# Middle heads of an attention kernel: third group's output product ahead of the eighth tile's transposes, the last exponential later, and the sparse row summed by VectorE

## The reference, cut to what matters

```python
scores = jnp.where(causal[None, None], -jnp.inf, scores)
probs = jax.nn.softmax(scores.astype(jnp.float32), axis=-1).astype(q.dtype)
attn = jnp.einsum('bhqk,bhkd->bhqd', probs, v)
...
io = sparse_out.mean(axis=2)[:, :, None, :VD]
io = jnp.broadcast_to(io, (B, IH, S, VD))
io = jnp.repeat(io, NH // IH, axis=1)
attn = attn + io
out = attn.transpose(0, 2, 1, 3).reshape(B, S, NH * VD) @ W_o
```

## Time and profile before

| what | value |
|---|---|
| runs | 697.52, 697.83, 703.88 us; median 697.83 |
| profiled execution | 697.48 us |
| its span, first to last instruction | 695.6 us |
| mean granted TensorE clock | 0.982 of full speed |
| busy | PE 94%, DVE 67%, ACT 58%, POOL 54% |
| chain that ended last | PE 62%, DVE 12%, ACT 11%, issue 9%, POOL 3%, DMA 1% |

### The profile page before, as it was taken

How to read it: one execution, slowest core, us unless ns; L and a number is a source line. 1 busy time by engine, 2 the same in 40 slices (tenths; PEclk the granted TensorE clock), 3 DMA queues, 4 the chain that set the end, 5 groups by cost and what they waited for, 6 DMA issues and landing times.

```text
span 695.6 us, 14180 instructions
## 1 busy us (share of the span) xinstructions
PE 654.3 (94%) x4502; PEld 594.1 (85%) x4502; DVE 467.7 (67%) x1292; ACT 400.5 (58%) x934; POOL 372.8 (54%) x335
## 2 busy tenths in 40 slices
PE   8897998999999999999999999999999999889895
PEld 6786987889888988898889888998899888779895
DVE  5884466666675657575756576666667667887986
ACT  4891346564656475736574476447664758545552
POOL 6882277245662757173826384448354735541564
PEclk9996999999999999999999999999999999999998
DMA  8307032510362034212441054104610383000001
GB/s 232 111 1 182 31 62 59 131 55 1 92 147 66 0 90 110 50 51 68 96 85 53 26 114 108 53 0 105 143 53 0 90 235 98 1 1 1 1 16 46
DMA packets 23551, 49.85 MB, mean 72 GB/s; under 512 B 3168, under 2 KB 16352, under 8 KB 21600
## 3 DMA queue, kind: packets, MB, share of 16 engines
q1 hardware_dynamic: 22144, 47.82, 27.4%
q10 hardware_dynamic: 1376, 1.64, 0.7%
HBM read 16.94 MB, written 1.05 MB: 26 GB/s over the span
## 4 chain that ended last, share of the span: by engine, by line
PE 62%; DVE 12%; ACT 11%; issue 9%; POOL 3%; DMA 1%; ACTq 0%; DVEq 0%; POOLq 0%; SPq 0%
PE J L840 10%; PE J L842 9%; PE J L841 9%; PE J L873 4%; PE SC L860 3%; ACT kvraw L1253 3%; PE SC L863 3%; PE SC L861 3%; PE SC L862 3%; PE SC L864 3%; DVE PTl L1299 3%; ACT Pb L1158 3%; POOL rstd L710 3%; PE SC L1054 2%; PE SC L1055 2%
## 5 line engine op out<-in xcount | busy, mean ns | idle before, releaser
L1299 DVE TENSOR_TENSOR PTl<-J,PTh 128x512 fp32r<-128x512 f32 (+1 forms) x192 | 102.2, 553 | 65.7 <-ACT PTh L1141 65.0
L1158 ACT ACTIVATE Pb<-SC,nm 128x128 f32<-128x128 f32 (+7 forms) x128 | 94.8, 741 | 63.3 <-DVE nm L1368 62.3
L1368 DVE CUSTOM_DVE_ANT_0 SC<-SC,mask 128x128 f32<-128x128 f32 (+7 forms) x128 | 97.3, 760 | 32.3 <-PE SC L864 30.4
L873 PE MATMUL J<-ident,Pb 128*128 128x128 f32 x576 | 87.4, 279 | 5.8 <-ACT Pb L1158 5.2
L1141 ACT ACTIVATE PTh<-J 128x512 fp32r<-128x512 f32 (+1 forms) x192 | 88.2, 491 | 7.5 <-PE J L873 6.7
L840 PE MATMUL J<-PTh,Vh 128*128 128x256 f32 x320 | 87.9, 275 | 2.8 <-DVE PTl L1299 2.8
L841 PE MATMUL J<-PTl,Vh 128*128 128x256 f32 x320 | 89.5, 280 | 0.0
L842 PE MATMUL J<-PTh,Vl 128*128 128x256 f32 x320 | 89.4, 279 | 0.0
L873 PEld LDWEIGHTS J<-ident,Pb 128*128 128x128 f32 x576 | 64.4, 142 | 13.2 <-ACT Pb L1158 6.7
L860 PE MATMUL SC<-KNh,QNh 128*128 128x128 f32 (+2 forms) x192 | 69.2, 360 | 0.1
L1141 ACT ACTIVATE ATh<-J 128x256 fp32r<-128x256 f32 x64 | 24.5, 383 | 73.7 <-PE J L842 72.9
(11 more groups left out here) (310 smaller groups left out, 1912.5 us busy)
## 6 DMA issues: line engine op xcount, KB each, us to landing
KK<-RK SPq DMA_DIRECT2D x30, 512.0 KB, 6.3
QS<-RQh SPq DMA_DIRECT2D x15, 256.0 KB, 6.2
QS<-RQl SPq DMA_DIRECT2D x15, 256.0 KB, 6.1
KX<-KX SPq DMA_DIRECT2D x14, 256.0 KB, 2.3
QX<-QX SPq DMA_DIRECT2D x14, 256.0 KB, 2.4
r_kv<-in_W_ckv SPq DMA_DIRECT2D x7, 384.0 KB, 3.3
r_o<-in_W_o SPq DMA_DIRECT2D x18, 128.0 KB, 3.3
r_qn<-in_W_qT SPq DMA_DIRECT2D x16, 128.0 KB, 3.2
```

The costliest lines, as they stand in the source:

```text
L873: last = pe.transpose(o[:, tile(j - 4 * c)], Pb[i % 2][:, tile(j)], ident[:, :])
L1158: act.activation(Pb[i % 2][:, w], SC[i % 2][:, s], ACT.Exp, bias=nm[:, i % 2:i % 2 + 1], scale=-1.0, accum_out=sm[:, b, i:i + 1]).then_inc ...
L1299: dve.tensor_tensor(o, i, h.bitcast(F32), ALU.subtract).then_inc(done[kind], 1)
L1368: dve.tensor_tensor_reduce(out=SC[i % 2][:, s], in0=SC[i % 2][:, s], in1=mask[:, 128 * (7 - i):S], scale=-SCALE, scalar=HIGH, op0=ALU.add, ...
```

## The change

1. `wo` 2 of the head before stands ahead of `tc` 7 (slot 0), in every head that has one before it.
2. In odd heads of the loop (`more and not first`) the second half of the query projection, `qp` 1, moves ahead of `pv` 3.
3. In the odd heads of FIRST and MID tile 7's `exp` stands one step later, behind `pv` 2.
4. In the same odd heads of MID the second `kt` moves from the end of slot 3 to slot 4, behind `wo` 0.
5. The row product leaves PE. DVE does `row = r_o * iocol + row` in one instruction per head, element by element, on W_o as it was loaded, one partition per row of `W_o`; it no longer needs the split in high and low parts. Once, in head 15, one fp32 matmul with ones (`rwt`) sums the 128 partitions, and a DVE copy brings the result back. ("skip") keeps the bank turns. SP's `W_o` load waits for the DVE instruction two heads before; POOL's split waits for `ab` alone, and two splits that nobody reads are gone. `io` and `rw` stand earlier in the odd heads.

```diff
@@ -370,7 +367,8 @@
-            add(0, tail, *t(m, 7), ("wo", m, 2))
+            add(0, tail, ("wo", m, 2), *t(m, 7))
+            add(1, b == 1 and more and not first, ("qp", 1, 1))
             add(1, tail, ("pv", m, 3))
...
@@ -382,7 +380,7 @@
-                add(4, True, *t(h, 3), ("wo", h, 0), ("rw", n, 0))
+                add(4, True, *t(h, 3), ("wo", h, 0), ("rw", n, 0), ("skip", 0, 0))
...
@@ -396,12 +394,13 @@
                 add(0, last, ("rw", 3, 0))
+                add(1, last, ("rwt", 0, 0))
...
-                add(1, more and not first, ("qp", 1, 1), ("ropeq", 1, 0))
+                add(1, more and not first, ("ropeq", 1, 0))
...
@@ -409,19 +408,19 @@
-                add(3, more and not first, ("kt", n, 1))
                 add(3, first, ("ab", n, 0), ("kvn2", 1, 0))
                 add(4, True, *t(h, 3), ("wo", h, 0))
-                add(4, more and not first, ("ab", n, 0))
+                add(4, more and not first, ("kt", n, 1), ("ab", n, 0))
...
-                add(6, more and not first, ("io", 1, 0))
+                add(4, more and not first, ("io", 1, 0))
                 add(6, True, *t(h, 5), ("wo", h, 1))
-                add(6, more, ("rw", n, 0))
+                add(5, more, ("rw", n, 0))
+                add(6, more, ("skip", 0, 0))
...
@@ -429,7 +428,7 @@
-            exp_at = [[2, 2, 2, 2, 2, 2, 2, 2], [2, 2, 2, 2, 2, 2, 2, 2]]
+            exp_at = [[2, 2, 2, 2, 2, 2, 2, 2], [2, 2, 2, 2, 2, 2, 2, 3 if more else 2]]
...
@@ -569,7 +568,8 @@
-                    wait(sp, wo_split, u)
+                    wait(sp, wo_split, min(u, NH) if isinstance(u, int) else u)
+                    wait(sp, rw_done, u - 2)
...
@@ -730,9 +730,8 @@
-                    if kind == "wosp" and not (isinstance(u, int) and u == 0):
-                        hold(gp, ready["ab"], min(u, NH) if isinstance(u, int) else u)
-                        split(ld_o, 16 * u + 16, r_o[:, :], Woh[:, :], Wol[:, :], wo_hi, wo_split, ready["rw"], u - 2, u)
+                    if kind == "wosp" and not (isinstance(u, int) and u in (0, NH, NH + 1)):
+                        split(ld_o, 16 * u + 16, r_o[:, :], Woh[:, :], Wol[:, :], wo_hi, wo_split, ready["ab"], u, u)
...
@@ -1006,10 +1005,9 @@
-                if kind == "rw":
-                    pe.wait_ge(io_ready, p + off // 2)
-                    pe.wait_ge(wo_split, u + 1)
-                    last = three(o[:, 0:D], iocol[:, 0:1].to_broadcast([128, 128]), iocol[:, 1:2].to_broadcast([128, 128]), Woh[:, :], Wol[:, :], True, True)
+                if kind == "rwt":
+                    pe.wait_ge(rw_done, NH)
+                    last = mm(o[:, 0:D], lhsT=onesf[:, :], rhs=row[:, :], start=True, stop=True)
...
@@ -1530,20 +1528,21 @@
-                            dve.tensor_copy(ioThl[:, :, 0], ioT[:, :]).then_inc(io_hi, 1)
-                            dve.wait_ge(io_hi, 1)
-                            dve.tensor_tensor(ioThl[:, :, 1], ioT[:, :], ioThl[:, :, 0].bitcast(F32), ALU.subtract).then_inc(io_hi, 1)
-                            dve.wait_ge(io_hi, 2)
-                        pair = ioThl[:, bass.ds(u, 1), :].rearrange("p a n -> p (a n)")
-                        dve.tensor_copy(iocol[:, :], pair.bitcast(F32)).then_inc(io_ready, 1)
+                        dve.tensor_copy(iocol[:, :], ioT[:, bass.ds(u, 1)]).then_inc(io_ready, 1)
...
                     if kind == "rw":
-                        dve.wait_ge(ready["rw"], count("rw", u, 0))
-                        dve.tensor_tensor(row[:, :], o[:, 0:D], row[:, :], ALU.add).then_inc(done["rw"], 1)
+                        dve.wait_ge(io_ready, p + off // 2)
+                        dve.wait_ge(ld_o, 16 * u + 16)
+                        if not (isinstance(u, int) and u == 2):
+                            hold(dve, rw_done, u - 2)
+                        dve.scalar_tensor_tensor(row[:, :], r_o[:, :], iocol[:, 0:1], row[:, :], ALU.mult, ALU.add).then_inc(rw_done, 1)
+                    if kind == "rwt":
+                        dve.wait_ge(ready["rwt"], 1)
+                        dve.tensor_copy(row[:, :], o[:, 0:D]).then_inc(done["rwt"], 1)
                     if kind == "rowadd":
-                        dve.wait_ge(done["rw"], NH)
+                        dve.wait_ge(done["rwt"], 1)
```

More of the change, by code:

```diff
@@ L123, in attention_and_mlp @@
         ioT = sb("ioT", [128, IH])
-        ioThl = sb("ioThl", [128, IH, 2], F32R)
-        iocol = sb("iocol", [128, 2], F32R)
+        iocol = sb("iocol", [128, 1])
         row = sb("row", [128, D])
@@ L246, in attention_and_mlp @@
                  ("qc", "qm", "kv", "kpe", "qp", "qps", "kt", "ab", "qn", "pv", "wo", "side", "tc", "wb",
-                  "rw", "wtot", "ht", "h2")}
+                  "rwt", "wtot", "ht", "h2")}
         hi = {k: sem(f"{k}_hi") for k in ("xs", "kt", "ab", "qn", "vs", "pv", "tc", "ht", "h2",
@@ L253, in attention_and_mlp @@
                 ("xs", "qc", "qm", "kv", "kpe", "qp", "qps", "kt", "ab", "qn", "vs", "pv", "wo", "side", "tc",
-                 "wb", "rw", "wtot", "ht", "h2")}
+                 "wb", "rwt", "wtot", "ht", "h2")}
         ld_mlp = [sem(f"ld_mlp{n}") for n in range(3)]
@@ L283, in attention_and_mlp @@
         tp_ready, pt_lo = ready["tc"], done["tc"]
-        io_hi, io_ready = sem("io_hi"), sem("io_ready")
+        io_ready, rw_done = sem("io_ready"), sem("rw_done")
         row_added = sem("row_added")
@@ L303, in unit @@
         def unit(kind, off, p):
-            if kind in ("wtot", "ht"):
+            if kind in ("wtot", "ht", "rwt"):
                 return off
@@ L1161, in run @@
                         kind, o = "qm", J[bank_of[("qm", 0, c)]]
-                    if kind in ready and not (kind in ("side", "wb", "wtot", "wo", "rw", "h2", "qc") or
+                    if kind in ready and not (kind in ("side", "wb", "wtot", "wo", "rwt", "h2", "qc") or
                                               kind in ("qp", "qps") and isinstance(u, int) and u == 0):
@@ L1532, in run @@
                             dve.wait_ge(done["side"], 13)
-                            dve.tensor_copy(ioThl[:, :, 0], ioT[:, :]).then_inc(io_hi, 1)
-                            dve.wait_ge(io_hi, 1)
-                            dve.tensor_tensor(ioThl[:, :, 1], ioT[:, :], ioThl[:, :, 0].bitcast(F32), ALU.subtract).then_inc(io_hi, 1)
-                            dve.wait_ge(io_hi, 2)
-                        pair = ioThl[:, bass.ds(u, 1), :].rearrange("p a n -> p (a n)")
-                        dve.tensor_copy(iocol[:, :], pair.bitcast(F32)).then_inc(io_ready, 1)
+                        dve.tensor_copy(iocol[:, :], ioT[:, bass.ds(u, 1)]).then_inc(io_ready, 1)
                     if kind == "io0":
-                        dve.wait_ge(ready["rw"], NH - 2)
-                        dve.tensor_copy(iocol[:, :], ioThl[:, 0, :].bitcast(F32)).then_inc(io_ready, 1)
+                        dve.wait_ge(rw_done, NH - 2)
+                        dve.tensor_copy(iocol[:, :], ioT[:, 0:1]).then_inc(io_ready, 1)
                     if kind == "rw":
-                        dve.wait_ge(ready["rw"], count("rw", u, 0))
-                        dve.tensor_tensor(row[:, :], o[:, 0:D], row[:, :], ALU.add).then_inc(done["rw"], 1)
+                        dve.wait_ge(io_ready, p + off // 2)
[6 more added lines that the diff above has]
+                        dve.tensor_copy(row[:, :], o[:, 0:D]).then_inc(done["rwt"], 1)
                     if kind == "rowadd":
-                        dve.wait_ge(done["rw"], NH)
+                        dve.wait_ge(done["rwt"], 1)
                         dve.wait_ge(done["wo"], count("wo", NH - 2, c))
```

4 lines of the change are left out of this document (1 added, 3 removed).

## The result

The changed kernel takes 713.58 us (median of 4 runs, 711.27 to 718.41), the kernel before in the same company 699.53. The ratio is 1.0204, with a 95% interval of 1.0156 to 1.0253: slower by 1.6 to 2.5%, and outside the range of 686 to 710 that was forecast. The profiled execution takes 714.28 us with a span of 712.4, 16.8 more than before. Its mean granted clock is 0.967 instead of 0.982.

What follows compares the result with a forecast made beforehand. PE was taken to bound the kernel; -5.7 - 2.9 + 11.1 + 0 + 1.8 + 1.8 + 0.7 - 1.1 = +5.7 on 697.5 gave 703.2 us, range 686 to 710.

Steps and rivals of the forecast that it cites:

- (c): Odd-to-even head boundary, seven times: `pv` 3 starts later behind `PTl` 7b, +1.58 us each, +11.1 for seven.
- (e): Boundaries head 0 to 1 and last pair: additions ahead of the chunk add about 0.9 us each, +1.8.
- The second rival: At the seven odd-to-even boundaries PE's new idle stretch lowers its clock: 12 us more, 715 us; chance 0.07.
- (a): Row product, 16 steps of three matmuls: it leaves PE, -5.7 us.
- (b): Odd heads: PE's wait at the row product goes with it, -2.9 us.
- (d): Even-to-odd boundary, six times: projection covers `pv` 3, 0; second `kt` in odd heads +0.3 us each, +1.8.
- (f): End of program: the one fp32 matmul with DVE's copy costs +0.7 us.
- (g): Head 1: DVE's cast `ioThl` and its follower go, so PE waits less, -1.1 us.
- (h): SP and POOL: changed waits and two splits fewer, 0, covered by PE.
- The rival on POOL: All 16 DVE row instructions held up by POOL, 0.7 us each: 11 us more, 714; chance 0.03.

Runs made afterwards that it cites:

- row sum, late: Kernel before with only the row sum moved to DVE, its row instruction in slot 6 instead of 5 in odd heads: 692.03 us, ratio 0.9864.
- row sum alone: Kernel before with only the row sum moved to DVE, its row instruction in slot 5 in odd heads: 693.60 us, ratio 0.9922.
- filled kernel: Changed kernel with 10 useless score matmuls of tile 1 in even heads from head 2 on: 703.73 us, ratio 1.0081.
- late row + `wo` + exponential: Kernel before with the row sum on DVE (slot 6 in odd heads), `wo` 2 ahead of tile 7's transposes and tile 7's exponential behind `ATh` in odd heads: 704.43 us.
- late row + projection: Kernel before with the row sum on DVE (slot 6 in odd heads) and the query projection's second half ahead of `pv` 3 in middle odd heads: ratio 0.9898.

## Why the prediction was wrong, point by point

**What failed is a term that the sum put at nothing: the clock behind the new wait.** Terms (c) and (e) price PE's idle stretch at its length alone. The second rival ("PE's new idle stretch lowers its clock", 715 us) got a chance of 0.07 and is what happened: about 1.5 us behind each of the seven boundaries, 10.5 us, and a low clock behind the two of (e) as well. The profiled execution takes 714.28.

The reason given against the rival was that PE is fuller here than in head 1. That was no evidence: nothing in the rows spoke for PE's fullness as a protection. Of the two waits that the prediction compared, 1.27 us with a full clock behind it and 2.58 with a low one, the forecast 2.2 was nearer to the second. But the length alone did not settle it either. The trace of the kernel before holds two more waits, and they go the other way round, the longer with a full clock behind it, the shorter with a low one (clock third from the end):

```profile
618.06 0.63 PE L873 MATMUL J<-ident,Pb 128*128 128x128 f32 x4 [1.64 <-ACT Pb L1158]
618.00:622.00 4.00, 3.94 (x29) 3.77 (x30) 3.83 (x9) 1.49 (x3) 0.09 (x1) 1.00 0.01 4
...
647.01 0.58 PE L1054 MATMUL SC<-QNh,xTh 128*128 128x256 f32 x1 [1.45 <-DVE CS L1463]
647.00:648.00 1.00, 0.99 (x4) 0.99 (x5) 0.97 (x5) 0.77 (x2) 0.52 (x1) 0.50 0.00 0
```

So the rows called for an open chance, near one half, and not for 0.07.

**What was right, and what was luck.** The turn was forecast at 73.6 us at full clock, and the changed kernel with its idle stretch filled takes 73.63. The boundary is right as a mechanism: from `pv` 2's last matmul to `pv` 3 it grew by 1.57 us, forecast 1.58. That the whole turn agrees to 0.03 is luck, for the parts miss by -0.34 to +0.22 and cancel.

| step | predicted | measured | from |
|---|---|---|---|
| (a), (b) row product and its waits, per turn | -1.10 | -0.88 | row sum, late: 71.92 against 72.80 |
| (c) `wo` and exponential, per turn | +1.58 | +1.24 | 73.16 against 71.92 |
| (d) projection, per turn | 0 | -0.01 | 71.91 against 71.92 |
| (d) second `kt`, per turn | +0.3 | +0.39 | 72.31 against 71.92 |
| low clock, per turn | 0 (rival: +1.7) | +1.5 | 75.12 against 73.63; 74.74 against 73.16 |
| (f) fp32 product | +0.7 | +0.25 | 626.51 to 626.76 |

The measured parts add up to -0.88 + 1.24 - 0.01 + 0.39 + 1.5 = +2.24 per turn, and the turn became 2.32 longer.

(c) The chain was as worked out: shifted by 2.03 us, so that `ATh` stands at 277.76 in both, the exponential was forecast for 278.03, 6a on DVE for 279.76, 7a for 282.08 and `pv` 3 for 283.39; the trace has 278.05, 279.76, 282.04 and 283.38. The wait came out at 1.61 and not 2.2: the bank wait ahead of the second four transposes takes some 0.45 of it (0.30 in the row, which counts idle time from the modelled end of a matmul, some 0.15 later than the end of its pitch), and the 1.61 is counted in the same way, 0.16 short. The turn grew by 1.24 and not by 1.58 because in the kernel it is compared with (row sum, late) the same stretch had already grown from 4.36 to 4.64. Of the 1.24, 0.77 are `wo` (72.69 against 71.92) and 0.47 the exponential on top (73.16 against 72.69). The shares of 0.27 and 0.22 against the row sum alone, which the expectation of the run with both started from, are too small, since there DVE's row instruction was still held up by POOL.

(d) With `wo` early as well, the filled kernel's 73.63 against 73.16 leaves 0.47 for `kt`, the projection and the earlier row instruction together, so the projection costs or gains next to nothing there too. The cover was worth little: where it is missing (late row + `wo` + exponential), `pv` 3 of even heads waits 0.37 us, not up to 1.0.

(e) In the last pair the wait grew from 1.27 to 2.43 us, 1.16 instead of 0.9, and the clock fell behind it too. The same happened at the boundary from head 0 to 1, behind a wait of 1.80. Together the two cost 4.7 us against the kernel with the row sum and the projection (2.4 in head 1, 2.3 from head 15 on), where 1.8 was forecast. These two and the seven are nine windows; two of the kernel before are gone (in head 1 and in the MLP), and one more lies in head 0, which appears in several of the other kernels as well.

(g) In head 1 the wait fell from 2.58 to 0.61, more than forecast, since DVE's second cast there (`iocol`, 0.98 us at 114.74), which the sum left out, became a copy of 0.14 (0.89 and 0.17 for the first cast and its follower, 0.84 for this: 1.90 of the 1.97); and the low clock behind it is gone. Head 1 takes 35.49 us with the row sum and the projection against 39.65 before. The changed kernel gives 2.4 of that back at the boundary 0 to 1 and takes 37.91.

(h) POOL and SP cost nothing here. The rival on POOL was right as a mechanism and wrong in its place: with the row instruction in slot 5 and nothing else moved, it takes 2.5 us in five odd heads of the loop and 1.31 in the first. The changed kernel escapes it, 1.03 at most. `wo` alone does that too, for with it DVE comes 0.20 us ahead of POOL's subtraction. The projection puts that subtraction 2.7 us earlier, which should be enough by itself, but no run has it alone with the row instruction in slot 5. The price where it happens is 0.50 per turn and not zero; the maximum of the next tile stands behind it. The slow cast that the prediction took as agreeing has one input, so it was no case of two inputs.

**A version that beats both kernels:** the row sum on DVE, late in odd heads, and nothing else of the change: 0.9864 of the time before (0.9786 to 0.9941). With the projection it is 0.9898, with `kt` 0.9901; the intervals of the three overlap, and by the turns the first two are equal and the third 0.4 us slower.

## What to carry to other kernels

When a new order opens an idle stretch on a PE that is otherwise full, price it twice: its length, and the time behind it at half clock. Collect all waits of the same trace with and without a low clock behind them, not one of each; where lengths of both kinds overlap, as 1.45 and 1.64 us do here, the chance is open, and only a run decides. Useless matmuls in the stretch are a cheap test of it. Where two moves each bring no low clock at the same boundary, test them together, since their delays add up on one chain: the waits of 1.22 and 0.26 us became one of 1.61. Take the price of a move from a kernel in which nothing else hides it. And keep DVE instructions with two inputs from SBUF out of the time of long POOL reads.

## What the runs showed that I had not expected

- Ten useless matmuls per turn make the kernel 10.5 us faster in span. Ahead of `pv` 3, in all fourteen traces, waits of up to 1.46 us never had a low clock behind them (1.01 to 1.31 at the seven boundaries, 1.45 and 1.46 in the last pair of the six kernels without part 1), waits of 1.79 and more always did, and waits of 1.61 to 1.70 did at seven boundaries of seven in one kernel and at two of seven in another. In other places the order does not hold: 1.64 us at 618.06 of the kernel before had none, 1.45 at 647.01 had one, and in head 14 two kernels (row sum alone; row sum, late) had one behind waits of 0.56 and 0.38 us, which a third (late row + projection) has as well, at full clock.
- One DVE instruction took 0.48 or 2.50 us by its place alone: issued 0.17 us behind POOL's subtraction of 2.38 us it takes 2.50, issued 0.20 us ahead of it 0.48. The Trainium skill, page "SBUF — State Buffer", section "Who interferes with whom", says that a DVE instruction with two SBUF inputs contends with a POOL instruction that reads SBUF, and that the order of issue decides which is blocked. The traces agree.
- An fp32 matmul of 256 columns took 0.25 us from its start to the next instruction's, against 0.12 for a product of the same width in the other format.
